# Splitting the up projection's weights as a seventh part, with a staging buffer of three parts

## The reference

```
for i in range(DEPTH):                                   # 6
    x = attn_layer(shift_tokens(x), Wqkv[i], ...) + x    # 16 heads of 64, window 32, l2-normed q, k, rotary
    x = ffn_layer(shift_tokens(x), ..., W1[i], b1[i], W2[i], b2[i]) + x
# ffn_layer: layer norm, hg = xn @ W1 + b1; a, gate = split(hg); (a * gelu(gate)) @ W2 + b2
```

## Time and profile before

| | us |
|---|---|
| median of the runs shown (3) | 1497.31 |
| the profiled execution's own time | 1497.48 |
| its span, first to last instruction | 1495.7 |
| PE busy | 1449.7 |
| DVE busy | 1348.3 |
| ACT busy | 1275.3 |
| POOL busy | 1245.6 |
| PE's part of the chain that ended last | 88% |

### The profile page before, as it was taken

One profiled execution on the slowest core, in us unless ns is written; L12 is line 12 of the kernel. 1 busy time (PEld: TensorE's weight loads), 2 busy tenths in 40 slices (PEclk: granted clock), 3 DMA queues, 4 the chain that ended last, 5 costly groups with the idle time before them and its releaser, 6 DMA issues.

```text
span 1495.7 us, 67060 instructions
## 1 busy us (share of the span) xinstructions
PE 1449.7 (97%) x26608; PEld 1290.8 (86%) x26608; DVE 1348.3 (90%) x2418; ACT 1275.3 (85%) x2605; POOL 1245.6 (83%) x1214
## 2 busy tenths in 40 slices
PE   6699999999999999999999999999999999999997
PEld 5578898889888888888898888889888988988886
DVE  7699999999999999999999999999999999999974
ACT  4577988888888898898889888888988888888886
POOL 5489988888899889898888898888889888888871
PEclk9999999999999999999999999999999999999999
DMA  6111122111122211221211122121212111211211
GB/s 162 43 42 50 49 59 63 45 49 53 47 54 66 70 37 40 62 63 51 76 43 41 49 57 74 53 61 35 59 36 65 44 45 40 56 49 35 52 46 28
DMA packets 96187, 80.31 MB, mean 54 GB/s; under 512 B 66282, under 2 KB 79598, under 8 KB 95854
## 3 DMA queue, kind: packets, MB, share of 16 engines
q1 hardware_dynamic: 94990, 75.34, 18.8%
q10 hardware_dynamic: 864, 0.26, 0.1%
HBM read 17.91 MB, written 1.05 MB: 13 GB/s over the span
## 4 chain that ended last, share of the span: by engine, by line
PE 88%; issue 4%; DVE 3%; ACT 3%; POOL 1%; DMA 1%; SPq 0%; ACTq 0%; POOLq 0%; DVEq 0%
PE bank L1140 70%; PE bank L1254 11%; PE bank L1292 5%; PE bank L1224 1%; ACT pz L725 1%; DVE parts L944 1%; PE bank L1326 1%; DMA rot<-in_b_v 0%; ACT sq L663 0%; ACT ot L732 0%; DVE n L954 0%; DVE w_lo L1026 0%; DVE s L990 0%; POOL rot L487 0%; POOL rot L476 0%
## 5 line engine op out<-in xcount | busy, mean ns | idle before, releaser
L476 POOL TENSOR_TENSOR rot<-parts 128x512 f32<-128x512 f32 x384 | 492.1, 1288 | 35.4 <-DVE parts L944 33.4
L944 DVE TENSOR_TENSOR parts<-bank,rtab 128x1024 f32<-128x1024 f32 x384 | 458.7, 1200 | 7.7 <-ACT sq L663 7.4
L487 POOL TENSOR_TENSOR rot<-rot,rnorm 128x512 f32<-128x512 f32 x384 | 394.6, 1043 | 12.0 <-DVE rnorm L970 12.0
L493 POOL TENSOR_TENSOR es<-es,r 128x512 f32<-128x512 f32 x192 | 200.4, 1044 | 151.8 <-DVE r L996 151.7
L954 DVE TENSOR_REDUCE n<-sq 128x8 f32<-128x512 f32 x384 | 259.1, 675 | 16.5 <-ACT sq L663 16.5
L1140 PE MATMUL bank<-w_hi,x_hi 128*128 128x512 f32 x576 | 265.6, 461 | 4.0 <-DVE parts L944 2.6
L663 ACT ACTIVATE sq<-bank 128x512 f32<-128x512 f32 x384 | 232.1, 604 | 18.5 <-PE bank L1140 6.9
L725 ACT ACTIVATE pz<-bank 64x512 f32<-64x512 f32 x384 | 225.9, 588 | 5.4 <-PE bank L1292 1.9
L1140 PE MATMUL bank<-w_lo,x_hi 128*128 128x512 f32 x576 | 228.5, 397 | 0.0
L1140 PE MATMUL bank<-w_hi,x_lo 128*128 128x512 f32 x576 | 228.0, 396 | 0.0
L1254 PE MATMUL bank<-ident,rot 128*128 128x128 f32 x1536 | 208.5, 273 | 10.7 <-DVE x_tok L1040 5.0
(11 more groups left out here) (95 smaller groups left out, 2901.9 us busy)
## 6 DMA issues: line engine op xcount, KB each, us to landing
vb<-v SPq DMA_DIRECT2D x96, 384.0 KB, 4.4
w_new<-in_Wqkv SPq DMA_DIRECT2D x36, 256.0 KB, 4.0
vb<-v SPq DMA_DIRECT2D x48, 128.0 KB, 2.3
w_o<-in_Wo SPq DMA_DIRECT2D x12, 256.0 KB
xin<-x_tok SPq DMA_DIRECT2D x48, 64.0 KB
xs<-x_tok SPq DMA_DIRECT2D x48, 64.0 KB, 2.0
xin<-x_tok SPq DMA_DIRECT2D x48, 56.0 KB
xs<-x_tok SPq DMA_DIRECT2D x48, 56.0 KB, 2.3
```

Source lines behind the costliest of these rows:

```text
L476: g.tensor_tensor(rot[:, i * CH:(i + 1) * CH].rearrange(halves, z=2, c=HD), parts[:, b:b + CH].rearrange(halves, z=2, c=HD), parts[:, b + ...
L487: g.tensor_tensor(c, c, over(r, CHH, DH), ALU.mult).then_inc(s_sc[i], 1)
L493: g.tensor_tensor(e, e, over(r8[:, (u % 2) * PAIRS:(u % 2 + 1) * PAIRS], PAIRS, DH), ALU.mult)\
L944: d.tensor_tensor(parts[:, b:b + 2 * CH].rearrange("p (w h c) -> p w h c", w=2, c=DH), heads(bank[QK_BANK[i]][:, :]).unsqueeze(1).to_broad ...
```

## The change

The number of weight parts per layer becomes seven (`WPARTS = WCH + 1`). Part 6 is the up projection's W1: ACT's `split_hi` and POOL's `split_lo` take it like any chunk, in the first sequence of the next layer's eight (`next_hi`, `next_lo` now run for seven sequences). `w1_hi` and `w1_lo` hold two layers. ACT's `up_hi` and DVE's `up_lo` are removed. `w_new` shrinks from 3072 to 1706 columns: two places of 512 for the QKV chunks by turns, and one of 682 for W1. So SP loads a chunk only when the chunk two before it has been split. Beside this, orders and banks change:

```diff
-V_BANK, P_BANK, O_BANK = (3, 6, 5, 0), (4, 6, 7, 4), (2, 6, 7, 4)
+V_BANK, P_BANK, O_BANK = (4, 6, 5, 0), (4, 6, 7, 4), (2, 6, 7, 4)
-XIN_BANK, N_BANK, D_BANK = 0, 4, 0
-LAST_N2, LAST_SC = (3, 7), (1, 4)
+XIN_BANK, N_BANK, D_BANK = 0, 3, 0
+LAST_N2, LAST_SC = (3, 7), (1, 6)
...
-        w_new = sb("w_new", QKV)
+        w_new = sb("w_new", 2 * CH + 2 * HID)
-        w1_hi = sb("w1_hi", 2 * HID, F32R)
-        w1_lo = sb("w1_lo", 2 * HID, F32R)
+        w1_hi = sb("w1_hi", 2 * 2 * HID, F32R)
+        w1_lo = sb("w1_lo", 2 * 2 * HID, F32R)
...
+        def chunk(l, c):
+
+            if c < WCH:
+                return slice((c % 2) * CH, (c % 2 + 1) * CH), slice((l % 2) * QKV + c * CH, (l % 2) * QKV + (c + 1) * CH)
+            return slice(2 * CH, 2 * CH + 2 * HID), slice((l % 2) * 2 * HID, (l % 2 + 1) * 2 * HID)
...
             def qkv_weights(l, c):
-                sp.wait_ge(s_wl, max(0, (l - 1) * WCH + c + 1))
-                if c < 2 and l != 2:
-                    sp.wait_ge(s_upl, max(0, l - 1) if l > 1 else l)
-                w = slice(c * CH, (c + 1) * CH)
-                sp.dma_start(w_new[:, w], Wqkv[l * P:(l + 1) * P, w]).then_inc(s_wq[c], 16)
+                sp.wait_ge(s_wl, max(0, l * WPARTS + c - 1 if c > 1 else (l - 1) * WPARTS + c + 5))
+                sp.dma_start(w_new[:, chunk(l, c)[0]], Wqkv[l * P:(l + 1) * P, c * CH:(c + 1) * CH]).then_inc(s_wq[c], 16)
 
             def up_weights(l):
 
-                if l < DEPTH - 1:
-                    sp.wait_ge(s_wl, (l + 1) * WCH + 2 if l else 2)
-                else:
-                    sp.wait_ge(s_upl, l)
-                sp.dma_start(w_new[:, 0:2 * HID], W1[l * P:(l + 1) * P, :]).then_inc(s_up, 16)
-
-            for c in range(WCH):
+                sp.wait_ge(s_wl, l * WPARTS)
+                sp.dma_start(w_new[:, chunk(l, WCH)[0]], W1[l * P:(l + 1) * P, :]).then_inc(s_wq[WCH], 16)
+
+            for c in range(2):
                 qkv_weights(0, c)
+            up_weights(0)
...
-            up_weights(0)
-            for c in (2, 3, 4, 5, 0, 1):
+            for c in range(2, WCH):
+                qkv_weights(0, c)
+            for c in range(2):
                 qkv_weights(1, c)
+            up_weights(1)
...
             def later_qkv(n):
-                if k == 2 and l > 0:
-                    up_weights(l)
-                for c in ((), (), (), (2,), (3,), (4,), (5, 0), (1,))[k]:
-                    if l + 2 < DEPTH:
-                        qkv_weights(l + 2, c)
+                if 1 <= k < WCH - 1:
+                    if l + 1 < DEPTH:
+                        qkv_weights(l + 1, k + 1)
+                elif k and l + 2 < DEPTH:
+                    if k <= WCH:
+                        qkv_weights(l + 2, k - WCH + 1)
+                    else:
+                        up_weights(l + 2)
```

```diff
                 if live(n - 1):
-                    freed((s_sub[0], n - 2, 4, 2))
+                    freed((s_hm[2], n - 5), (s_pte[0], n - 2, 4, 0))
                     project_v(n - 1, 0)
...
-                    freed((s_hm[2], n - 5), (s_pte[0], n - 2, 4, 0), (s_ot[3], n - 3))
+                    freed((s_sub[0], n - 2, 4, 2), (s_mid[0], n - 3), (s_xg, n - 5))
                     turn_normal(n - 4)
...
-                    freed((s_v[0], n - 1))
+                    freed((s_xg, n - 4), (s_sub[0], n - 2, 4, 2))
                     turn_qk(n - 1, 3)
...
-                    freed((s_xg, n - 4), (s_pte[0], n - 2, 4, 0))
+                    freed((s_v[0], n - 1), (s_hm[2], n - 5), (s_pte[0], n - 2, 4, 0))
                     turn_p(n - 2, 3)
```

More of the change, by code:

```diff
@@ L29 @@
 WCH = QKV // CH
+WPARTS = WCH + 1
 MASKED = -1.0e30
@@ L460, in split_lo @@
             def split_lo(l, c):
-                pool.wait_ge(s_wh, l * WCH + c + 1)
-                f, w = slice(c * CH, (c + 1) * CH), slice((l % 2) * QKV + c * CH, (l % 2) * QKV + (c + 1) * CH)
-                g.tensor_tensor(w_lo[:, w], w_new[:, f], w_hi[:, w].bitcast(F32), ALU.subtract).then_inc(s_wl, 1)
+                pool.wait_ge(s_wh, l * WPARTS + c + 1)
+                new, w = chunk(l, c)
+                hi, lo = (w_hi, w_lo) if c < WCH else (w1_hi, w1_lo)
+                g.tensor_tensor(lo[:, w], w_new[:, new], hi[:, w].bitcast(F32), ALU.subtract).then_inc(s_wl, 1)
             def next_lo(n):
                 c = n % SEQS - SPLIT_FROM
-                if 0 <= c < WCH and layer(n) < DEPTH - 1:
+                if 0 <= c < WPARTS and layer(n) < DEPTH - 1:
                     split_lo(layer(n) + 1, c)
@@ L510, in normalise @@
                 last.then_inc(s_xn, 1)
-            def first_up_lo():
-                pool.wait_ge(s_uph, 1)
-                g.tensor_tensor(w1_lo[:, :], w_new[:, 0:2 * HID], w1_hi[:, :].bitcast(F32), ALU.subtract)\
-                 .then_inc(s_upl, 1)
-            for c in range(WCH):
+            for c in range(WPARTS):
                 split_lo(0, c)
-            first_up_lo()
             def iteration(n):
@@ L541, in iteration @@
                 if live(n - 2):
+                    divide(n - 2, 2)
                     divide(n - 2, 3)
@@ L548, in iteration @@
                     scale(n - 1, 7)
-                    scale(n - 1, 5)
+                    scale(n - 1, 4)
                 if live(n):
@@ L616, in split_hi @@
                     last = (l - 1) * SEQS - 1
+                    if c == WCH:
+                        for j in range(HCH):
+                            act.wait_ge(s_hid[j], done(last))
                     for k in range(2):
@@ L619, in split_hi @@
                             act.wait_ge(s_qk[c + 4 * k], done(last))
-                        else:
+                        elif c < WCH:
                             act.wait_ge(s_vp[c - 4 + 2 * k], done(last))
-                f, w = slice(c * CH, (c + 1) * CH), slice((l % 2) * QKV + c * CH, (l % 2) * QKV + (c + 1) * CH)
-                a.activation(w_hi[:, w], w_new[:, f], ACT.Copy).then_inc(s_wh, 1)
+                new, w = chunk(l, c)
+                a.activation((w_hi if c < WCH else w1_hi)[:, w], w_new[:, new], ACT.Copy).then_inc(s_wh, 1)
             def next_hi(n):
                 c = n % SEQS - SPLIT_FROM
-                if 0 <= c < WCH and layer(n) < DEPTH - 1:
+                if 0 <= c < WPARTS and layer(n) < DEPTH - 1:
                     split_hi(layer(n) + 1, c)
-            def split_up(l):
-                act.wait_ge(s_up, 16 * (l + 1))
-                for j in range(HCH):
-                    act.wait_ge(s_hid[j], l * SEQS)
-                a.activation(w1_hi[:, :], w_new[:, 0:2 * HID], ACT.Copy).then_inc(s_uph, 1)
-            def up_hi(n):
-                if n % SEQS == SEQS - 1 and layer(n) < DEPTH - 1:
-                    split_up(layer(n) + 1)
             for s in range(-1, SEQS + 1):
                 first_attention(s)
-                if 0 <= s < WCH:
+                if 0 <= s < WPARTS:
                     split_hi(0, s)
-                if s == WCH:
-                    split_up(0)
             act.wait_ge(s_late, 16 * NLATE)
@@ L1020, in xg_lo_part @@
                  .then_inc(s_xg, 1)
-            def up_lo(n):
-                if n % SEQS == SEQS - 1 and layer(n) < DEPTH - 1:
-                    dve.wait_ge(s_uph, layer(n) + 2)
-                    d.tensor_tensor(w1_lo[:, :], w_new[:, 0:2 * HID], w1_hi[:, :].bitcast(F32), ALU.subtract)\
-                     .then_inc(s_upl, 1)
             def gated(n, j):
@@ L1095, in iteration @@
                     moments(n - 4)
+                if live(n - 1):
+                    newton_half(n - 1, 0)
                 if live(n - 3):
@@ L1098, in iteration @@
                 if live(n - 1):
-                    newton_half(n - 1, 0)
                     squares(n - 1, 4)
```

36 lines of the change are left out of this document (13 added, 23 removed).

## The result

The changed kernel takes 1488.87 us (median of 4 runs, 1488.56 to 1490.45), the kernel before 1496.99 us beside it: ratio 0.9949, 95% interval 0.9931 to 0.9966. That is 8.1 us less, where 7.7 were forecast, and 0.7 us under the predicted time. Measured again in five more runs with the last experiment it had 1491.08 us (1489.22 to 1491.72), ratio 0.9957 (0.9943 to 0.9970). So the gain is 6.5 to 8 us; the forecast lies between the two medians. The profiled execution took 1488.56 us, its span 1486.8.

The account below looks back on a forecast made before the run. TensorE, busy 1449.7 of 1495.7 us, was taken as the bound. Gains of 6.6 (boundary passes), 0.45 (start) and 0.7 (fill) made 7.75 us; 1497.5 less that is 1489.7, stated as 1489.6 us, range 1486.5 to 1494.0.

Parts of the forecast that it names:

- Up projection split: Five layer-boundary passes: with the late split off VectorE and ScalarE they become ordinary 29.20 us passes, gaining 6.6 us.
- Delay minus slack is the stall: Boundary passes: TensorE's 0.99 us wait for `finish` is the late split's delay less half a microsecond of slack.
- Where the split goes: First pass of a layer: 0.76 us more on ScalarE and 1.68 us on GpSimd fit their idle time, cost 0.
- Staging: Weight loads in three parts: each waits for the chunk two before, yet lands well before use, cost 0.
- own mark for a misread steady state: Ordinary passes stay at 29.18 to 29.20 us; 0.05 us or more off means a prediction wrong by 43 times that.
- Prologue: Program start: one weight load instead of two ahead of the first input load gains 0.45 us; chunk 2's lateness costs 0.
- Order of GpSimd: Filling passes: `divide(2)` behind `add(6)` and `scale(1)` readies the scale 3 us earlier, closing TensorE's 0.78 us gap; 0.7 us gained.
- Rival 2: TensorE's swapped order: issue stalls move, 0.24 us for one more group per pass, 11.5 us slower, 1501; 4 in 100.
- Banks and TensorE's order: TensorE's exchanged projection, transposes and banks: same instructions, new waits already met by earlier ones, cost 0.
- newton_half: VectorE, now ahead of `middle`: `middle` ends near 605.95 instead of 604.66, scores' slack shrinks to 0.35-0.4 us, cost 0.

Follow-up runs that it names:

- split_only: The changed kernel with the banks and the GpSimd, VectorE and TensorE orders of before; seventh part and three-part staging kept: 1488.20 us, ratio 0.9938.
- orders_only: The kernel before with only the changed banks and GpSimd, VectorE and TensorE orders, the up projection's split left where it was: 1498.22 us, ratio 1.0005.
- late_lo: The changed kernel with the low half of the up projection's weights made on VectorE at the layer boundary again: 1491.76 us, ratio 0.9969.
- twice_seventh: The changed kernel with the seventh part made twice for layers 1 to 5, on GpSimd and on ScalarE: 1491.58 us, ratio 0.9962.
- after_again: The changed kernel itself, unaltered, timed and profiled once more against the kernel before: 1491.08 us, ratio 0.9957.
- shift8: The changed kernel with 4 tiny matmuls (8 instruction slots) ahead of the output projection in the fourth iteration alone: 1487.47 us, ratio 0.9937.
- shift32: The changed kernel with 16 tiny matmuls (32 slots) in the fourth iteration and in that of the last sequence's stopping scores: 1487.93 us, ratio 0.9939.
- pool_old: The changed kernel with GpSimd's order of before alone (divide(2) ahead of add(6); scale(5), scale(6), scale(4)): 1488.45 us, ratio 0.9947.
- warm_more: The changed kernel with 42 unused identity transposes in TensorE's early gaps and 43 more meant for its waits in the fill: 1489.50 us, ratio 0.9952.
- pe_warm: The changed kernel with 42 unused identity transposes in TensorE's idle gaps between 46 and 54 us: 1489.41 us, ratio 0.9951.

## Why the prediction was right, step by step

The largest term was right in mechanism and size; that the total came so near is luck. In the profiles the span fell by 8.9 us, against 7.75 in the sum: the start gave 1.3 us more than its term, the ordinary passes 1.75 us and the end 0.9 us that no term had, and the fill missed its term by 2.9 us the other way.

**Up projection split, -6.6.** Right: the five boundary passes fell by 6.69 us in sum. What would be late next was read rightly as nothing. `split_only` and `orders_only` show that this edit alone makes the gain. "Delay minus slack is the stall" holds in four kernels, with 0.4 us of slack where half a microsecond was read; of the delay of 1.7 us before, 0.66 are ScalarE's copy and the rest VectorE's subtraction (table at `late_lo`), which stands four instructions ahead of `finish`, not three. The size of the stall was partly chance: the same subtraction takes 1.20 or 0.86 us by what GpSimd does beside it.

**Where the split goes, 0.** Right, but the thinner cover is on ScalarE, to which the working gave one clause: GpSimd has over 1.4 us to spare, ScalarE some 0.35 us (`twice_seventh`).

**Staging, 0.** No wait appears. The ordinary passes are 0.05 us shorter with the new split and staging in every profile, 1.75 us over 37. The cause stays open. It isn't that SP issued two weight parts in one pass: the four passes in which it did are only 0.02 us longer before than after, while those of a layer's sequence 2, in which it issued none, are 0.13 us longer on average. The prediction took 29.20 us for an ordinary pass of the kernel before, whose average is 29.23; the average after, 29.18, lies in the 29.18 to 29.20 that it named. Its own mark for a misread steady state (0.05 us a pass) is just met between the two kernels, and 1.75 us are missing from the sum.

**Prologue, -0.45.** The term itself is right. From the end of GpSimd's last split to the start of the first input's last transfer it is 3.45 us in the profiles with the old split (`orders_only` as well) and 2.93 to 2.95 in those with the new one (after, `split_only`, `late_lo`, `after_again`). Chunk 2 was not late. Of the rest of the table's -1.76, 0.9 us come from a last split that ended sooner (46.14 against 47.03) and 0.35 from a shorter input transfer (2.85 against 3.20). Neither is shown to belong to the change: in `after_again`, the same kernel, the split ends at 46.76 and sequence 0 starts at 52.73. The landing of the value bias doesn't explain it either: 10.40 us before and 9.43 after, but 9.42 in `after_again` and 9.48 in `orders_only`, whose last split ends at 46.84.

**Order of GpSimd, -0.7.** This step failed. The 0.78 us gap did go, but nothing was gained by it: the five filling passes became 2.2 us longer (0.8 in `after_again`), and 2.2 in `orders_only`. The step looked at one wait and not at what TensorE meets next: the second scores of sequence 1 now start 2.5 us earlier (1.8 of it because sequence 0 does), while the transfer of their block of instructions starts 1.5 us later than before; they stop 1.8 us, and 3.5 us at 1.2 GHz follow. Rival 2 named the right kind of event, issue stalls that move, but placed it in every pass. `shift8` is the test of this: 8 instruction slots more, the stop is gone, and the fill is 114.12 us, 2.8 less. `shift32` gives the same (114.29) and removes the last sequence's stop as well. Three things stay open. What makes TensorE ask for a block: `pool_old` has the same TensorE program as after and its transfer starts 3.5 us earlier. What the rest of the loss is: `split_only` has no stop and a fill 1.3 us longer than before. And what GpSimd's order alone costs or gives: the fill of `pool_old` lies between the two profiles of the change, which are 1.4 us apart.

**Banks and TensorE's order, 0.** Right for the steady passes (`split_only`: 1225.6 us against 1225.4).

**`newton_half`, 0.** The sum's 0 holds. The forecast that `middle` would end 1.3 us later does not: `newton_half` came first (602.55, GpSimd's sum L481 at 602.56) and took 0.16 us, the other branch of the same step. Its rule (the Trainium skill, SBUF — State Buffer, Who interferes with whom: whichever of the two starts first holds the shared ports) agrees with both lengths, 1.17 us in the earlier trace rows and 0.16 us after. As forecast, VectorE's microsecond was hidden by TensorE.

**The end, not in the sum.** Its -0.92 us is within what two executions of the changed kernel differ by there (92.34 and 93.49 us).

## What to carry to other kernels

When a pass is longer than its neighbours and TensorE is busy in the neighbours, moving late work to where two other engines have slack can give the whole difference, as it did here; measure that slack on both, as it was 0.35 us on one and over 1.4 on the other. Where two delays share one slack, count each by how far it moves the instruction that is waited for, not by what is left when the other is gone. A gap closed in a filling pipeline is not yet a gain: ask what the engine behind it reaches earlier. In a long program of short instructions list each pause without a releaser beside the instruction transfers; if the restarts follow them at a like distance, a few dummy instructions ahead of the place are a cheap test. Here they gave the lowest median, 1487.47 us, though the ratios don't tell it from `split_only` or `shift32`. And look in the timeline whether dummy work fills a wait or stands behind it, as in `warm_more`.

## What the hardware showed that was not expected

- Instructions come in 16 KB transfers while the program runs (242 on q8), and where one started between 0.55 us ahead and 0.7 us behind the start of a scores group of 136 short matmuls, TensorE stopped in that group, 0.53 to 2.09 us. In 22 stops over 14 profiles the restart was 2.15 to 2.88 us after a transfer's start. Where it started 1.03 us ahead or more, there was no stop.
- After the stop of 1.82 us the granted clock was 0.51 (1.2 GHz) from 113.5 to 117 us, and the pass behind it was 0.9 us longer than in `shift8`; in `after_again`, whose stop was 1.54 us, it stayed 1.00 (114 to 117.5) and the next pass was as short as in `shift8` (26.10 us).
- Dummy work kept TensorE at 2.4 GHz from 44 to 62.3 us (`pe_warm`), and the third pass started at the same time, since VectorE set it.
- A subtraction of 128x682 on VectorE took 1.20 us where it began during an instruction of GpSimd and 0.86 us where GpSimd was idle.
- An early 64 KB input took 2.63 to 3.39 us, and a bias landed between 9.03 and 10.40 us, with no edit that would explain it; a microsecond in a program's start should not be read from one profile.
